# Block-sparse attention scores: six half-array matmuls over interleaved key parts become four whole-array matmuls over planes stacked in device memory

## The chip, the cores and the metric

The kernel runs on one core of one Trainium2 chip. Its time is device microseconds of one execution. Before the change, three runs took 908.22 us (median), 907.25 and 910.98 us.

## The reference, cut to what matters

One transformer layer on x of shape (16, 512, 128), float32: attention with 16 heads of 8 channels, then a mixture of four experts.

```python
qkv = (x @ qkv_w.T).reshape(B, N, 3, H, HD).transpose(2, 0, 3, 1, 4)    # x is layer-normed; H=16, HD=8, N=512
qb, kb = mean of q, k over blocks of 64 rows                            # M=8 blocks
c = einsum('bhmd,bhnd->bhmn', qb, kb) * SCALE
block_mask = (c >= top-1 of c) | eye(M)                                 # each query block sees its own and its best block
scores = where(mask, einsum('bhqd,bhkd->bhqk', q, k) * SCALE, -inf)
out = softmax(scores) @ v;  x = x + out @ proj_w.T + proj_b
x = x + experts(layernorm(x))      # 4 experts, hidden 512, top 2 by a router, gelu, gates by softmax
```

So each query block of 64 rows meets 128 keys: 64 of its own block and 64 of one selected block. Per batch row that is 8 blocks, each with 16 heads.

## The kernel before, in words

The 16 batch rows ("batches", b) are worked on in a software pipeline. During batch b's eight attention blocks m, TensorE also computes q, k and v for batch b+1 (`project`, L275), the router of b-1 (`c_route`) and the down projections of the experts of b-2 (`c_down`, L396: two chunks a block, numbers 2m and 2m+1). After block 7 come the sixteen up projections of the experts of b-1 (`c_up`), and behind number 13 of them `begin(b+1)` puts the first scores of the next batch. Everything is placed by hand: each engine has its program in order, and semaphores join them.

One block on TensorE goes: `weighted` (probabilities times values, L346), `row_max` (two transposes of block maxima, L326), `scores(b, m+1)` (L310), `shift` (16 small bf16 matmuls that add minus the row maximum, L335), other work, the `c_down` chunks (L403), `values(b, m+1)` (a transpose, L319). In blocks 0 and 7 chunk 2m stands ahead of the next scores and of the shift; in blocks 1 to 6 both chunks come near the end. `scores` of a block waits on the gelu of the bank that it overwrites for m below 2, and on the exponentials else. VectorE follows with `block_max` (L672, two a block) and `row_max` (L681), ScalarE with the exponential (L940), the gelus (L976) and copies.

Precision: q and k are each split into a high and a low float32r part, and a score is high*high + low*high + high*low. Before, `kv` holds for each channel (h, d) on its own partition, for 128 keys, three values side by side: high k, low k, v. `qdiag` holds q block-diagonally: partition (h, d) has numbers only in the columns of head h, eight heads to a half of the array. `scores` runs three products for each half: six matmuls with 64 partitions and 512 columns. SyncE places q with 32 DMAs a batch (`place_q`, L1143), 16 KB each.

The keys travel as follows. ScalarE and VectorE write k high, k low and v into `stage`. SyncE stores it in device memory as `table` (L1136) and copies it into the own half of `kv` (L1140). VectorE finds the best block (`a_select`) and writes row numbers (`index`, L647); GpSimd gathers those rows from `table` into `selected` (L1050); SyncE writes them to `chosen` (L1157) and reads them back, permuted, into the other half of `kv` (L1164). For batch 0 GpSimd gathers straight into `kv` with eight indirect DMAs (L1059), one a block, each with a semaphore of its own. SyncE runs all its DMAs in program order, and a wait in it holds what stands behind.

Of the kernel before, what the change touches and what calls it, by code (L numbers as in the profile page):

```python
# [32 lines left out]
ROW = 3 * BS  # L33
# [29 lines left out]
def layer(nc, x, wqkv_t, wproj_t, proj_b, w1, b1_t, w2, b2, wr, br, ident, head_sum,  # L63
          head_one, block_rank, row_mine, row_base, lane_base, expert_before, expert_rows, own_block, head_mask,
          query_rows, key_rows, out):
    with ExitStack() as ctx:
# [23 lines left out]
        rbase, lbase = sb("rbase", [P, 1]), sb("lbase", [P, 1])  # L90
# [18 lines left out]
        qdiag = [sb(f"qdiag{g}", [P, 2, HH, N // 2], F32R) for g in range(2)]  # L109
        stage = [sb(f"stage{i}", [P, M, BS, 3], F32R) for i in range(2)]  # L110
        kv = [sb(f"kv{i}", [P, M, KEYS, 3], F32R) for i in range(2)]
# [11 lines left out]
        first_index = sb("first_index", [P, M], U32)  # L123
# [49 lines left out]
        gates = [nc.dram_tensor(f"gates{b}", [E * T, P], F32, kind="Internal").ap() for b in range(B)]  # L173
        constant = nc.dram_tensor("constant", [E, D], F32, kind="Internal").ap()
# [10 lines left out]
        table_out = [sem(f"table_out{i}") for i in range(2)]  # L185
        own_in = [sem(f"own_in{i}") for i in range(2)]
        gathered, sel_out = sem("gathered"), sem("sel_out")
        sel_in = [sem(f"sel_in{i}") for i in range(2)]
        first_in = [sem(f"first_in{m}") for m in range(M)]
# [5 lines left out]
        constant_out = sem("constant_out")  # L195
# [34 lines left out]
        second = [(hsum, head_sum), (rank, block_rank), (mine_of, row_mine), (rbase, row_base), (lbase, lane_base), (wproj, wproj_t),  # L230
# [5 lines left out]
        PLACED = H * 16  # L236
# [7 lines left out]
        def taken(b):  # L244

            return 16 * (times(b, 2) - (1 if b % 2 == 0 else 0))
# [10 lines left out]
        def tensor(pe):  # L257
# [33 lines left out]
            def scores(b, m):  # L291
                j, i, u = b % 2, m % 2, b * M + m
                if m % HALF == 0:
                    pe.wait_ge(q_placed[m // HALF], PLACED * (b + 1))
                if m == 0:
                    pe.wait_ge(own_in[j], 16 * times(b, 2))
                    if b >= 1:
                        pe.wait_ge(sel_in[j], taken(b))
                if b == 0:
                    pe.wait_ge(first_in[m], 16)  # L300
                if m < 2 and b >= 2:
                    pe.wait_ge(gelued, UPS * (b - 2) + (UP_SPREAD if m == 0 else UPS))
                elif u >= 2:
                    pe.wait_ge(exped, u - 1)
                for n in range(3):
                    for half in range(2):
                        r = slice(half * P // 2, (half + 1) * P // 2)
                        keys = kv[j][r, m, :, 1 if n == 2 else 0]
                        queries = qdiag[m // HALF][r, 1 if n == 1 else 0, :, m % HALF * BS:(m % HALF + 1) * BS]
                        ins = pe.matmul(s_ps[i][:, half * N:(half + 1) * N].rearrange("p (h s) -> p h s", s=BS), keys, queries,  # L310
                                        start=n == 0, stop=False, skip_group_check=True)
                        if n == 2:
                            ins.then_inc(scored, 1)

            def values(b, m):
                was = bank_v.next("values", b, m)
                if was:
                    pe.wait_ge(bank_v.free, was)
                pe.transpose(v_ps[:, 0:P], kv[b % 2][:, m, :, 2].bitcast(F32), idn[:]).then_inc(bank_v.full, 1)  # L319
# [144 lines left out]
            for b in range(B):  # L464
                ahead = b >= 1 and b + 1 < B
                for m in range(M):
# [27 lines left out]
                    if b >= 2 and not edge:  # L494
                        c_down(b - 2, 2 * m)
# [64 lines left out]
        def vector(v):  # L560
# [39 lines left out]
            def a_q_parts(b):  # L600
                if b >= 1:
                    for g in range(2):
                        v.wait_ge(q_placed[g], PLACED * b)
# [3 lines left out]
            def a_k_low(b):  # L607
                st, kview = stage[b % 2], block_ap(a_ps[:])
                v.wait_ge(k_high, b - 1)
                total = step(v.tensor_reduce(ksum[:], kview, AXX, ALU.add))  # L610
                v.tensor_tensor(st[:, :, :, 1], kview, st[:, :, :, 0].bitcast(F32), ALU.subtract).then_inc(bank_a.free, 1)
                return total

            def a_k(b, bank="a"):
                j, (of, src) = b % 2, banks[bank]
                st, kview = stage[j], block_ap(src[:])
                v.wait_ge(of.full, of.at["k", b])
                if b >= 2:
                    v.wait_ge(table_out[j], 16 * times(b - 2, 2))
                    v.wait_ge(own_in[j], 16 * times(b - 2, 2))  # L620
                hi = step(v.tensor_copy(st[:, :, :, 0], kview))
                total = step(v.tensor_reduce(ksum[:], kview, AXX, ALU.add))
                v.wait_ge(dve_step, hi)
                v.tensor_tensor(st[:, :, :, 1], kview, st[:, :, :, 0].bitcast(F32), ALU.subtract).then_inc(of.free, 1)
# [8 lines left out]
            def a_select(b):  # L633
# [11 lines left out]
                if b >= 3:  # L645
                    v.wait_ge(gathered, 16 * (b - 2))
# [3 lines left out]
            def a_select_first():  # L650
                v.wait_ge(bank_a.full, bank_a.at["products", 0])
                v.tensor_scalar(crow[:].rearrange("p m n -> p (m n)"), a_ps[:, 0:M * M], 1.0 / (BS * BS), SCALE,
                                ALU.mult, ALU.mult).then_inc(bank_a.free, 1)
                v.wait_ge(bank_a.free, bank_a.at["products", 0])
                v.wait_ge(dve_step, step(v.tensor_reduce(cmax[:], crow[:], AXX, ALU.max)))
                v.wait_ge(dve_step, step(v.tensor_tensor(ceq[:], crow[:], heads_of(cmax[:]).broadcast_to([P, M, M]), ALU.is_ge)))
                counted = step(v.tensor_reduce(cties[:], ceq[:], AXX, ALU.add))
                ranked = step(v.tensor_tensor(crow[:], ceq[:], rank[:].rearrange("p (o n) -> p o n", o=1).broadcast_to([P, M, M]),
                                              ALU.mult))
                v.wait_ge(dve_step, ranked)  # L660
                v.wait_ge(dve_step, step(v.tensor_reduce(crank[:], crow[:], AXX, ALU.max)))
                v.tensor_scalar(first_index[:], crank[:], -float(P), lbase[:], ALU.mult, ALU.add).then_inc(index_done, 1)
                v.wait_ge(dve_step, counted)
                return step(v.tensor_reduce(ties[:, 0:1], cties[:], AXX, ALU.max))
# [145 lines left out]
            a_rows(1)  # L810
# [3 lines left out]
            a_q_parts(0)  # L814
            v.tensor_copy(idn16[:], idn[:]).then_inc(dve_set, 1)
            v.wait_ge(attention_in, SECOND)
            tied = a_select_first()
# [88 lines left out]
        def scalar(act):  # L906
# [6 lines left out]
            def a_v(b, bank="a"):  # L913
                j, (of, src) = b % 2, banks[bank]
# [642 lines left out]
```

## Time and profile before

| | us |
|---|---|
| median of three runs | 908.22 |
| profiled execution | 907.23 |
| its span, first to last instruction | 905.6 |
| TensorE busy | 861.6 (95%) |
| VectorE busy | 523.0 (58%) |
| ScalarE busy | 469.8 (52%) |
| GpSimd busy | 181.8 (20%) |
| DMA moved | 99.40 MB, 96021 packets |
| mean granted TensorE clock | 0.987 |

Busy time of TensorE is modelled from pipelined matmuls, so a stretch in which it is always busy need not be one in which it works at its peak. The chain of waits is the better guide: it gives each microsecond of the span to the instruction that the end waited for. The rows themselves stand in a section further down. The first scores of batch 0 start 28.26 us into the span, and after batch 1 every batch takes the same time.

### The profile page before, as it was taken

What the parts mean: (1) busy time and instruction counts of PE and PEld (TensorE: products, weight loads), DVE (VectorE), ACT (ScalarE), POOL (GpSimd) and SP (SyncE); (2) the same over time, 40 slices, a digit from 0 to 9 for tenths busy, and PEclk for the clock granted to TensorE, in tenths of its full rate; (3) what the DMA queues carried; (4) which work ended last, traced back from release to release, by engine and by line L of the source; (5) the groups of instructions that cost most, each with busy time, mean ns of one, the idle gap of its engine ahead of it and who ended that gap; (6) DMA issues with size and microseconds to landing.
All of it is one profiled execution on the core that took longest, in us unless ns stands there. A gap on an engine that the chain in (4) does not pass through costs nothing.

```text
span 905.6 us, 24229 instructions
## 1 busy us (share of the span) xinstructions
PE 861.6 (95%) x9638; PEld 578.9 (64%) x9638; DVE 523.0 (58%) x1525; ACT 469.8 (52%) x754; POOL 181.8 (20%) x183
## 2 busy tenths in 40 slices
PE   3887799999999999999999999999999999999995
PEld 2665576666667666666666666666766666666662
DVE  7545647565565756656474656556475755646321
ACT  1432374655547474654647465564746455473740
POOL 5701010312022121302112130312203130211111
PEclk9898999999999999999999999999999999999998
DMA  7440442425344351625435152534525262530110
GB/s 209 141 127 21 119 139 73 129 77 166 98 137 133 84 160 37 190 74 153 115 114 155 44 158 76 155 111 119 151 77 135 67 180 73 149 109 3 59 59 14
DMA packets 96021, 99.40 MB, mean 110 GB/s; under 512 B 8968, under 2 KB 82704, under 8 KB 95904
## 3 DMA queue, kind: packets, MB, share of 16 engines
q1 hardware_dynamic: 93168, 85.09, 33.6%
q0 software_dynamic: 2544, 12.58, 4.3%
q8 instruction: 78, 1.28, 0.6%
q14 instruction: 39, 0.32, 0.1%
q10 hardware_dynamic: 192, 0.13, 0.1%
HBM read 48.10 MB, written 28.71 MB: 85 GB/s over the span
## 4 chain that ended last, share of the span: by engine, by line
PE 88%; ACT 4%; DVE 3%; issue 1%; SPq 1%; DMA 1%; POOL 0%; POOLq 0%; DVEq 0%; ACTq 0%
PE y_ps L403 23%; PE s_ps L310 13%; PE o_ps L346 8%; PE s_ps L259 6%; PE s_ps L261 5%; PE s_ps L260 5%; PE s_ps L335 4%; ACT hid L976 4%; PE o_ps L353 4%; PE v_ps L326 3%; PE v_ps L319 2%; PE v_ps L365 2%; PE a_ps L376 2%; PE a_ps L268 2%; PE v_ps L403 2%; PE v_ps L360 2%
## 5 line engine op out<-in xcount | busy, mean ns | idle before, releaser
L403 PE MATMUL y_ps<-hid,w2s 128*128 128x512 f32 x480 | 235.1, 600 | 0.0
L672 DVE TRANSPOSE_TENSOR_REDUCE rmax<-s_ps 128x16 bf16<-128x512 f32 x256 | 168.9, 701 | 92.2 <-PE s_ps L310 89.8
L940 ACT ACTIVATE prob<-s_ps 128x1024 f32<-128x1024 f32 x128 | 131.3, 1026 | 173.6 <-PE s_ps L335 173.6
L976 ACT ACTIVATE hid<-s_ps,b1s 128x512 f32<-128x512 f32 x256 | 171.2, 689 | 36.9 <-PE s_ps L261 34.8
L310 PE MATMUL s_ps<-qdiag,kv 64*128 64x512 f32 x768 | 132.8, 451 | 1.9 <-DMA qdiag<-qpair 1.9
L1079 POOL TENSOR_TENSOR yT<-yT,gate_cols 128x512 f32<-128x512 f32 x48 | 61.5, 1282 | 304.1 <-DVE gate_cols L768 303.7
L259 PE MATMUL s_ps<-xnhi,w1hi 128*128 128x512 f32 x256 | 112.5, 439 | 1.5
L403 PEld LDWEIGHTS y_ps<-hid,w2s 128*128 128x128 f32 x480 | 83.0, 192 | 43.8 <-issue 40.0
L310 PEld LDWEIGHTS s_ps<-qdiag,kv 64*128 64x128 f32 x768 | 84.8, 252 | 28.4 <-ACT hid L976 10.6
L261 PE MATMUL s_ps<-xnhi,w1lo 128*128 128x512 f32 x256 | 100.9, 394 | 0.0
L681 DVE TENSOR_REDUCE nmax<-v_ps 128x64 bf16<-128x256 bf16 x128 | 54.0, 422 | 80.3 <-PE v_ps L326 79.7
L260 PE MATMUL s_ps<-xnlo,w1hi 128*128 128x512 f32 x256 | 100.3, 392 | 0.0
L346 PEld LDWEIGHTS o_ps<-prob,vaug 128*32 128x32 f32 x4096 | 63.4, 110 | 50.4 <-issue 37.1
L933 ACT COPY vaug<-v_ps 128x128 f32<-128x128 f32 x128 | 34.1, 266 | 117.3 <-PE v_ps L319 116.6
L346 PE MATMUL o_ps<-prob,vaug 128*32 128x64 f32 x4096 | 84.1, 223 | 0.1
L335 PEld LDWEIGHTS s_ps<-nmax,hone 64*128 64x128 bf16 x2048 | 37.5, 96 | 40.3 <-DVE nmax L681 22.9
L259 PEld LDWEIGHTS s_ps<-xnhi,w1hi 128*128 128x128 f32 x256 | 49.9, 195 | 18.9 <-ACT hid L976 8.8
L335 PE MATMUL s_ps<-nmax,hone 64*128 64x64 bf16 x2048 | 52.8, 192 | 3.5 <-DVE nmax L681 3.5
L948 ACT COPY oT<-o_ps 128x512 f32<-128x512 f32 x64 | 37.6, 587 | 34.9 <-PE o_ps L346 34.9
L261 PEld LDWEIGHTS s_ps<-xnhi,w1lo 128*128 128x128 f32 x256 | 48.0, 188 | 11.1
L260 PEld LDWEIGHTS s_ps<-xnlo,w1hi 128*128 128x128 f32 x256 | 48.5, 190 | 6.6 <-issue 0.7
L1041 POOL TENSOR_TENSOR xs<-xs,projb 128x512 f32<-128x512 f32 x16 | 20.5, 1282 | 140.2 <-DVE xn L579 140.2
(151 smaller groups left out, 1069.6 us busy)
## 6 DMA issues: line engine op xcount, KB each, us to landing
gate_cols<-gates SPq DMA_DIRECT2D x64, 256.0 KB, 4.3
kv_table<-stage SPq DMA_DIRECT2D x16, 768.0 KB, 3.9
kv<-stage SPq DMA_DIRECT2D x16, 768.0 KB
kv_chosen<-selected SPq DMA_DIRECT2D x15, 768.0 KB, 5.1
kv<-kv_chosen SPq DMA_DIRECT2D x15, 768.0 KB, 5.0
qdiag<-qpair SPq DMA_DIRECT2D x504, 16.0 KB
xs<-in_x SPq DMA_DIRECT2D x16, 256.0 KB, 5.6
out_x<-x SPq DMA_DIRECT2D x16, 256.0 KB, 5.9
```

The lines of the kernel that those rows point to most:

```text
L259: pe.matmul(dst, left_hi, right_hi, start=True, stop=False)
L260: pe.matmul(dst, left_hi, right_lo, start=False, stop=False)
L261: return pe.matmul(dst, left_lo, right_hi, start=False, stop=True)
L310: ins = pe.matmul(s_ps[i][:, half * N:(half + 1) * N].rearrange("p (h s) -> p h s", s=BS), keys, queries, start=n == 0, stop=False, skip_g ...
L335: ins = pe.matmul(s_ps[i][:, half * N + h * BS:half * N + (h + 1) * BS], hone[r, h, :], nmax[i][r, :], start=False, stop=True, skip_group_ ...
L346: ins = pe.matmul(o_ps[32 * (h % HQ):32 * (h % HQ) + VW, h // HQ, i * BS:(i + 1) * BS], vaug[i][:, h, :], prob[i][:, h, :], start=True, st ...
L403: ins = pe.matmul(dst[:], w2s[:, n, :], hid[:, n, :], start=(c == 0), stop=(c == C - 1))
L672: v.tensor_reduce(rmax[m % 2][:, :, half * P // 2:half * P // 2 + HH].rearrange("p k h -> p h k"), s_ps[m % 2][:, half * N:(half + 1) * N] ...
L681: v.tensor_reduce(nmax[m % 2][:].rearrange("h (b c) -> h b c", b=2), v_ps[:, 0:P].bitcast(BF16).rearrange("h (b g c) -> h b c g", b=2, g=4 ...
L940: act.activation(prob[m % 2][:].rearrange("p h s -> p (h s)"), s_ps[m % 2][:], ACT.Exp, scale=SCALE).then_inc(exped, 1)
L976: act.activation(hid[:, k, :], up_ps[up_bank(k)], ACT.Gelu, bias=b1s[:, k:k + 1]).then_inc(gelued, 1)
L1079: g.tensor_tensor(yT[:], yT[:], gate_cols[(E * b + e) % NG][:], ALU.add).then_inc(summed, 1)
```

## The change

Each row of `table` gets four planes per channel instead of three interleaved values: high k, low k, high k, v, 64 numbers each. On partitions, a quad of four heads now stands as (head, channel, plane), 4*8*4 = 128 partitions. q gets matching planes (high, high, low, zero) in a new table in device memory, `qtab`, so one matmul with 128 partitions sums all three products of four heads. A block takes four matmuls (one per quad) of 256 columns. The q, k and v of batch b+1 go through device memory: `put_q`, `place_q` (8 DMAs a batch of 128 KB), `put_high` and `put_low` (table in two parts), `take_own` (own keys read back from `table`), `take_keys` in two halves and `take_values`. v is kept apart in `vals`. `stage` has one buffer instead of two. Batch 0 takes the same way as the others; its eight direct gathers go. In blocks 1 to 6 of batches 2 and up, chunk 2m of `c_down` moves to between `scores(b, m+1)` and `shift(b, m)`; in block 0 it moves from ahead of the scores to behind them. The constants `head_sum`, `row_mine` and `row_base` are relabelled for the new order of rows.

```diff
+PLANES = 4
+ROW = PLANES * BS
@@ scores
-                for n in range(3):
-                    for half in range(2):
-                        r = slice(half * P // 2, (half + 1) * P // 2)
-                        keys = kv[j][r, m, :, 1 if n == 2 else 0]
-                        queries = qdiag[m // HALF][r, 1 if n == 1 else 0, :, m % HALF * BS:(m % HALF + 1) * BS]
-                        ins = pe.matmul(s_ps[i][:, half * N:(half + 1) * N]..., keys, queries, start=n == 0, ...)
+                if m % HALF == 0:
+                    pe.wait_ge(sel_k_in[j][m // HALF], 16 * times(b, 2))
+                for g in range(QUADS):
+                    queries = qdiag[m // HALF][:, g, :, m % HALF * BS:(m % HALF + 1) * BS]
+                    ins = pe.matmul(s_ps[i][:, g * HQ * BS:(g + 1) * HQ * BS]..., keys[j][:, m, g, :],
+                                    queries, start=g % 2 == 0, ...)
@@ values: waits at m == 0
+                    pe.wait_ge(own_v_in[b % 2], 16 * times(b, 2))
+                    pe.wait_ge(sel_v_in[b % 2], 16 * times(b, 2))
@@ order of a block on TensorE
-                    edge = m in (0, M - 1)
-                    if b >= 2 and edge:
-                        c_down(b - 2, 2 * m)
                     if m + 1 < M:
                         scores(b, m + 1)
+                    if b >= 2:
+                        c_down(b - 2, 2 * m)
                     shift(b, m)
...
-                    if b >= 2 and not edge:
-                        c_down(b - 2, 2 * m)
@@ sync, new functions
+            def put_high(b):
+                s.wait_ge(k_high, b + 1)
+                s.dma_start(plane_of(table[b], ..., 0, 1), stage[:, :, 1, :]).then_inc(table_out, 16)
+            def put_low(b, of_k, of_v):
+                s.dma_start(plane_of(table[b], ..., 1, PLANES), stage[:]).then_inc(table_out, 16)
+                s.dma_start(vals[b % 2][:, :, 0:BS], stage[:, :, 2, :]).then_inc(own_v_in[b % 2], 16)
+            def take_own(b):
+                s.wait_ge(table_out, 2 * 16 * (b + 1))
+                s.dma_start(keys[b % 2]...[:, :, 0:BS], key_rows_of(table[b])).then_inc(own_k_in[b % 2], 16)
+            def put_q(b):
+                s.dma_start(into[:, 0, :], qhi).then_inc(q_out, 16)
+                s.dma_start(into[:, 1:3, :], qpair[:]).then_inc(q_out, 16)
+            def place_q(b, half):
+                s.wait_ge(q_out, 2 * 16 * (b + 1))
+                for h in range(HQ):
+                    s.dma_start(qdiag[half][r, :, h, :], qtab[b % 2]...[h][:, :, half * N // 2:(half + 1) * N // 2]
+                                ).then_inc(q_placed[half], 16)
+            def put_selected(b):
+                s.wait_ge(gathered, 16 * (b + 1))
+                for half in range(2):
+                    s.dma_start(chosen[b][r, :], selected[r, :]).then_inc(sel_out[half], 16)
+            def take_keys(b, half):
+                s.wait_ge(sel_out[half], 16 * (b + 1))
+                s.dma_start(keys[b % 2][:, half * HALF:(half + 1) * HALF, :, BS:]...,
+                            key_rows_of(chosen[b][half * P // 2:(half + 1) * P // 2, :])).then_inc(sel_k_in[b % 2][half], 16)
+            def take_values(b):
+                s.dma_start(vals[b % 2][:, :, BS:], plane_of(chosen[b], ..., PLANES - 1, PLANES)).then_inc(sel_v_in[b % 2], 16)
+            def take_selected(b):
+                take_keys(b, 0)
+                take_values(b)
+                take_keys(b, 1)
@@ sync, order for batch b + 1 where b >= 1
+   put_q, put_high, place_q(half 0), put_low, take_own, put_selected, take_selected, place_q(half 1)
@@ sync, order for batch 0
+   q_null x2, load(third), put_high, put_low, put_q, take_own, place_q(half 0), put_selected, take_selected, place_q(half 1)
@@ vector, before the loop
+            v.memset(prob[0][:, 0:HH, :], 0.0).then_inc(null_set, 1)
-            a_rows(1)
             total = a_k(0, "y")
...
-            tied = a_select_first()
+            tied = a_select(0)
+            a_rows(1)
@@ scalar, before the loop
-            for h in range(HH, H):
-                act.dma_start(qdiag[0][r, :, h % HH, :], qpair[r, :, 0:N // 2]).then_inc(q_placed[0], 16)
@@ pool, before the loop
-            a_select_first()
+            a_select(0)
```

## Rows read from the trace of the kernel before

**Rows 1.** The page's chain of waits: shares of the span by engine

```profile
PE 88%; ACT 4%; DVE 3%; issue 1%; SPq 1%; DMA 1%; POOL 0%; POOLq 0%; DVEq 0%; ACTq 0%
```

**Rows 2.** Windows, one batch each: us, busy by engine, clock, DMA share, GB/s

```profile
439.00:491.00 52.00, 51.87 (x598) 34.62 (x598) 31.82 (x94) 29.20 (x48) 10.04 (x10) 1.00 0.42 118
491.00:543.00 52.00, 51.87 (x598) 34.63 (x598) 31.92 (x94) 29.21 (x48) 10.03 (x10) 1.00 0.41 118
```

**Rows 3.** Chain of waits in one batch, TensorE's pieces: start us, us, what

```profile
438.69 0.96 PE s_ps L310 x6
439.65 0.32 PE v_ps L319
...
441.49 0.91 PE y_ps L403 x2
442.40 0.96 PE s_ps L310 x6
443.36 0.25 PE s_ps L335 x16
...
447.82 0.54 PE a_ps L376 x4
...
453.56 0.23 PE a_ps L260
...
455.74 0.11 PE v_ps L319
...
476.81 0.34 PE s_ps L335 x16
```

**Rows 4.** ScalarE's timeline in that batch: start us, us, line, operation

```profile
440.70 1.38 ACT L976 ACTIVATE hid<-s_ps,b1s 128x512 f32<-128x512 f32 x2 [0.43 <-PE s_ps L261]
442.10 1.28 ACT L940 ACT_TABLE_LOAD   x1
```

**Rows 5.** VectorE's timeline in block 3 of that batch

```profile
459.73 0.69 DVE L610 TENSOR_REDUCE ksum<-a_ps 128x8 f32<-128x512 f32 x1 [0.77 <-ACT stage L926]
...
461.91 0.41 DVE L681 TENSOR_REDUCE nmax<-v_ps 128x64 bf16<-128x256 bf16 x1
```

**Rows 6.** Timelines of SyncE's queue and of GpSimd, same batch

```profile
465.59 0.36 SPq L1136 DMA_DIRECT2D kv_table<-stage  x1
...
476.59 0.58 SPq L1157 DMA_DIRECT2D kv_chosen<-selected  x1
...
483.81 0.38 SPq L1164 DMA_DIRECT2D kv<-kv_chosen  x1
...
471.03 1.11 POOL L1050 DMA_INDIRECT selected<-kv_table,index  x1 [7.69 <-DVE index L647]
```

**Rows 7.** Windows around single transfers, columns as in rows 2

```profile
6.00:8.00 2.00, 0.49 (x3) 0.52 (x4) 2.00 (x9) 0.00 (x0) 0.21 (x1) 1.00 0.27 54
441.00:447.00 6.00, 5.96 (x77) 3.79 (x77) 3.08 (x9) 4.13 (x6) 1.22 (x1) 1.00 0.87 259
...
472.00:476.00 4.00, 4.00 (x64) 2.64 (x63) 3.36 (x14) 1.29 (x2) 1.72 (x3) 1.00 0.71 224
477.00:482.00 5.00, 5.00 (x62) 3.54 (x55) 3.15 (x16) 4.28 (x7) 1.67 (x3) 1.00 0.65 167
...
18.00:23.00 5.00, 3.11 (x11) 2.98 (x12) 2.94 (x11) 0.00 (x0) 0.88 (x1) 1.00 1.02 311
```

**Rows 8.** The page: median us from issue to landing

```profile
kv_table<-stage SPq DMA_DIRECT2D x16, 768.0 KB, 3.9
...
kv<-kv_chosen SPq DMA_DIRECT2D x15, 768.0 KB, 5.0
```

**Rows 9.** Chain of waits at the start

```profile
10.02 5.08 DVE xn L579 x4
15.10 0.74 DVE stage L621
...
28.26 1.15 PE s_ps L310 x4
```

**Rows 10.** Windows of batches 0 and 1, columns as in rows 2

```profile
28.30:68.00 39.70, 35.86 (x548) 26.33 (x548) 22.46 (x52) 15.09 (x26) 12.51 (x14) 0.91 0.48 133
68.00:127.50 59.50, 47.94 (x595) 36.60 (x594) 33.29 (x114) 27.12 (x46) 8.73 (x11) 0.91 0.31 84
```

More of the change, by code:

```diff
@@ L242, in stages, with key_rows_of, plane_of @@
             return (2, 0, 1, 3) if b == 0 else (2, 3, 4, 5)
-        def taken(b):
-            return 16 * (times(b, 2) - (1 if b % 2 == 0 else 0))
+        def key_rows_of(dram):
+            return dram[:, :].rearrange("(n q) (r s) -> (q r) n s", q=HQ, s=BS)
+        def plane_of(dram, pattern, first, last):
+            return dram[:, :].rearrange(pattern, n=M, d=HD)[:, :, first * BS:last * BS]
         def heads_of(ap):
@@ L318, in values @@
                     pe.wait_ge(bank_v.free, was)
[L319 removed]
+                if m == 0:
+                    pe.wait_ge(own_v_in[b % 2], 16 * times(b, 2))
+                    pe.wait_ge(sel_v_in[b % 2], 16 * times(b, 2))
+                pe.transpose(v_ps[:, 0:P], vals[b % 2][:, m, :], idn[:]).then_inc(bank_v.full, 1)
             def row_max(b, m):
@@ L1155, in put_selected @@
-            def put_selected(b):
-                s.wait_ge(gathered, 16 * b)
-                s.dma_start(chosen[b][:, :].rearrange("(m h) c -> h m c", m=M), selected[:]).then_inc(sel_out, 16)
-            def take_selected(b):
-                j = b % 2
-                s.wait_ge(sel_out, 16 * b)
+                s.dma_start(vals[b % 2][:, :, 0:BS], stage[:, :, 2, :].bitcast(F32)).then_inc(own_v_in[b % 2], 16)
+            def take_own(b):
+                s.wait_ge(table_out, 2 * 16 * (b + 1))
+                if b >= 2:
+                    s.wait_ge(scored, 2 * M * (b - 1))
+                s.dma_start(keys[b % 2][:].bitcast(F32).rearrange("p m g k -> p (m g) k")[:, :, 0:BS],
+                            key_rows_of(table[b])).then_inc(own_k_in[b % 2], 16)
@@ L1162, in take_selected @@
+            def take_values(b):
+                for half in range(2):
+                    s.wait_ge(sel_out[half], 16 * (b + 1))
                 if b >= 2:
                     s.wait_ge(bank_v.full, bank_v.at["values", b - 2, M - 1])
-                s.dma_start(kv[j][:, :, BS:, :].bitcast(F32).rearrange("p m s c -> p m (s c)"),
-                            chosen[b][:, :].rearrange("(m h) (d c) -> (h d) m c", m=M, d=HD)).then_inc(sel_in[j], 16)
+                s.dma_start(vals[b % 2][:, :, BS:],
+                            plane_of(chosen[b], "(n h) (d c) -> (h d) n c", PLANES - 1, PLANES)).then_inc(sel_v_in[b % 2], 16)
@@ L1193, in sync @@
             load(second, attention_in)
+            s.wait_ge(null_set, 1)
+            for q_rows in qtab:
+                s.dma_start(q_rows.rearrange("(p t) c -> p t c", t=PLANES)[:, 3, :],
+                            prob[0][:, 0:HH, :].rearrange("p h s -> p (h s)")).then_inc(q_null, 16)
             load(third, experts_in)
-            a_v(0, bank_y, bank_v)
-            place_q(0, 0, range(HH))
-            place_q(0, 1, range(H))
+            put_high(0)
+            put_low(0, bank_y, bank_v)
+            put_q(0)
+            take_own(0)
+            place_q(0, 0)
+            put_selected(0)
+            take_selected(0)
+            place_q(0, 1)
             for b in range(B):
```

199 lines of the change are left out of this document (83 added, 116 removed).

## The prediction

> **What bounds the kernel now.** I read the chain of waits first: 88% of the span is TensorE's [rows 1]. Then the windows: from batch 2 on, a batch takes 52.0 us with TensorE busy throughout at the full granted clock, while VectorE and ScalarE work 32 and 29 us and DMA fills 0.42 of its time [rows 2]. So in the fourteen batches 2 to 15 a microsecond taken from TensorE is one gained, unless another engine or a transfer then comes late. Batches 0 and 1 (39.7 and 59.5 us) are looser and run partly at half clock [rows 10]. Ahead of them lie 28.3 us of start, in which TensorE waits for data [rows 9]. That gives three terms: start, batches 0 and 1, and fourteen steady batches.
>
> **Scores on TensorE.** Six half-array matmuls cost 0.96 us on the chain [rows 3]. The new four have 256 columns each, on all 128 partitions. No row shows that shape. From below: a full matmul of 512 columns costs 0.23 us when its weights load behind the one before (L260) [rows 3], and half the columns give 0.115, so 0.46 for four. From above: nothing gained, 0.96, if loads no longer hide. Four records that are almost nothing but a weight load (4 columns) take 0.54 us, 0.135 each (L376) [rows 3]. So load and stream are about equally long here; I take 0.125 a matmul, 0.50, and 0.09 for the first, whose load nothing hides behind the short transposes of `row_max`: 0.59. That saves 0.37 a block.
>
> **The chunk ahead of the shift.** It costs no work, but it parts two groups that both run on half arrays. The shift behind scores takes 0.25 us, behind a full-array chunk 0.34 [rows 3]: +0.09 in blocks 1 to 6. Net 0.28 x 6 = 1.68 us a batch. In exchange VectorE's row maximum has 1.45 us of cover instead of 0.96, and it needs about 0.5.
>
> The Trainium skill ("TensorEngine Tiling (Array Packing)", Key Properties) says that changing the tiling mode drains the array, which speaks against placing the chunk there. The row agrees in kind and prices it at 0.09 us. By the rule alone, without a figure, the sum would only be said to be smaller.
>
> **The first scores of a batch** stand between up projections, so their load hides: 0.50 for 0.96, and the transpose behind them needs no change of tiling, 0.11 for 0.32 [rows 3]. With block 0's second scores (-0.37 + 0.09) that is nominally 0.95 us. But `scores(b, 1)` overwrites the banks of the last gelus. These end at 442.08, and it started at 442.40 behind the chunk [rows 3, 4]. Now it comes first. The gelus move up by the 0.66 us that TensorE gained (last up projection 441.36 to 440.70), end at 441.43, and TensorE reaches the scores at 440.84. So 0.6 us of waiting appears, and the gain of this stretch is 0.35, not 0.95.
>
> **Block 3 to 4.** VectorE's `nmax` of block 4 starts at 461.91, delayed by the k sums, which started at 459.73 behind ScalarE's copy [rows 5], itself behind the exponential. The shift is later by the chunk (0.95) less 0.37, so that whole chain slides by some 0.6 us while the block gets shorter: shift 4 waits about 0.35 us more. In the other blocks the same sum leaves room.
>
> A steady batch: 1.68 + 0.35 - 0.35 = about 1.65 us less, 52.05 to 50.4. Bounds: 4.0 less if no wait appears and a matmul costs 0.115; 1.5 more if loads don't hide.
>
> **Transfers.** Price of a run, from engine time: 441 to 447 holds 3072 runs of 512 B, 6 x 0.87 x 16 / 3072 = 27 ns; 18 to 23 moves runs of 768 B at 311 GB/s, 39 ns; in 6 to 8 some 400 tiny runs come to about 9 ns each beside 128 of 512 B [rows 7]. Between them 256 B should cost about 18 ns; 9 and 27 are the bounds. Per batch: own keys 4096 runs, 4.6 us of all engines; selected keys the same in two halves; table, values and q some 8 us more. The busy share rises from 0.42 to about 0.66. That in itself costs nothing, but the last chain counts. Before, from the start of a batch (438.69): table written +26.9, gather +32.3, chosen written +37.9, read back +45.1 [rows 6], landed 5.0 later [rows 8] at +50.1; needed at +52.05. After: table +26.0, landed +30.2; own keys and gather (2.8 us of engine time for 0.79 MB, 4 x 0.71 [rows 7], so 3.8 for 1.05 MB) share the engines from +32 to +40.4; the chosen write (about 3.1 us of engine time, now 4.1 [rows 7]) lands by halves at +43.8 and +46; first keys +48.3, values +49.6. Needed at +50.4 and +50.9. It just fits, by 2.1 and 1.3 us. SyncE's waits: behind `take_own` wait q, `put_selected` and the gates; with 17 fewer DMAs a batch to issue (19 for 36) it is not the one that is late.
>
> **Start.** VectorE's a_rows(1) took 5.08 us ahead of the k split at 15.10 [rows 9]; moved behind it, k is ready from 11.5 and the index at about 19. The queue carries the weights and two q_null stores until 18. Then: table (1.3 + 2.5 us) at 22.3; own keys after values and q 25.5 to 30.5 with the gather; `place_q` 32; chosen 32 to 36, first half 34.5; keys 39.3, values 40. First scores at 39.5 instead of 28.26: +11.2 (bounds +7 and +18, by the price of a run). The direct gathers that go had let block 0 begin with an eighth of the keys.
>
> **Batches 0 and 1.** They have no chunk; 0.37 a block less, in part lost in waits at these clocks: -1.2 each (0 to -3).
>
> **Sum**, against the profiled execution of 907.2 (span 905.6 and 1.6 around it; 1.0 below the median): 907.2 + 11.2 - 2.4 - 14 x 1.65 = 892.9, so 893.
>
> **Rivals.**
> 1. *Late keys* (slower). With runs of 256 B at the price of 512 B (27 ns), own keys take 6.9 us, half the selected 3.5, values 1.7: +4.1 us, values at +53.7. TensorE then waits 2.8 us a batch, 53.2 us instead of 52.05: 907.2 + 8.8 + 14 x 1.15 = 932. It decides from a wait of 1.0 us a batch, where gain and start cancel. For it: the margin of 1.3 us is worked out, not seen. Against: two sizes and the tiny runs lie on one line.
> The Trainium skill ("DMA: Bandwidth & Descriptors", Specifications) gives 512 B as the least transfer at line rate, with read-modify-write below. This change cuts runs of 768 B into 256 B; no row here has enough of them to test it. By that rule this rival's price holds.
> 2. *Loads don't hide* (slower). Four times stream plus load, 0.115 + 0.115 each, is 0.92 and the scores gain nothing; with 0.09 x 6 and the waits, +1 a batch: 907.2 + 11.2 + 14 = 932. The row of 0.23 us for 512 columns speaks against it.
> The Trainium skill ("TensorE: Matmul & The Clock Gate", What overlaps and what doesn't) says that a weight load overlaps a matmul only where row groups differ. The up projections here, all on the full array, do overlap.
> 3. *All cover holds*: 0.46 a group, no new wait, 3 us a batch, start +9: 872.
> 4. *The gain turns into waits* of VectorE and ScalarE (the gelus and block 3 are two already), 0.5 to 0.9 us a batch: about 905.
>
> **Chances.** Forecast 0.42, late keys 0.24, loads 0.06, all cover 0.13, waits 0.15. Range 874 to 934; the likeliest case alone 883 to 902. About 0.5% is what can be told from no change: faster than 903.7 gets 0.42 + 0.13 + a fifth of rival 4 = 0.58, within 0.13, slower 0.29.
>
> **What would show it.** The scores group at 0.5 to 0.6 us; a wait of the first-block scores on a gelu of 0.6 us; the shift at 0.34; batch windows of 50.4 us; first scores near 39.5; DMA share near 0.66. I am wrong if a wait on `keys` or `vals` stands in the chain at each batch's begin, if the group stays near 0.96, or if the clock falls in those gaps.

## The result, and the profile after

| | median us | runs | lowest to highest |
|---|---|---|---|
| before, same chip | 909.23 | 4 | 907.25 to 910.98 |
| after | 925.58 | 4 | 918.75 to 930.87 |

The ratio is 1.0181, 95% interval 1.0146 to 1.0217: slower, by 1.5 to 2.2%. Forecast was 893, and faster. The profiled execution took 926.25 (span 924.6). First the page's chain of waits of the kernel after, shares of the span by engine, then its windows, one batch each (columns as in rows 2: us, busy by engine, clock, DMA share, GB/s).

```profile
PE 58%; DMA 26%; ACT 6%; DVE 4%; issue 3%; SPq 2%; POOL 0%; POOLq 0%; DVEq 0%; ACTq 0%
```

```profile
562.15:613.57 51.42, 50.01 (x581) 32.42 (x581) 31.71 (x94) 28.73 (x47) 10.04 (x10) 1.00 0.68 177
507.93:562.15 54.22, 52.80 (x580) 33.95 (x581) 31.80 (x94) 28.13 (x46) 10.04 (x10) 0.94 0.67 174
...
43.00:81.70 38.70, 34.49 (x533) 26.17 (x533) 21.84 (x52) 14.99 (x26) 0.97 (x1) 0.89 0.86 205
81.70:139.00 57.30, 45.43 (x570) 35.49 (x570) 33.01 (x112) 25.76 (x44) 8.73 (x11) 0.88 0.57 142
```

DMA is now 26% of the chain, from 1% [rows 1]. A share of the chain isn't time lost: it says what the end waited for, and most of that would have passed behind TensorE's work anyway. The steady batches take 51.4 to 51.8 us where keys are nearly or quite in time and up to 54.81 where they are late; before, all took 52.0 [rows 2]. TensorE is idle 1.4 us even in a good one. Measured from the first scores of one batch to those of the next, the span splits so:

| us | before | after | difference | forecast |
|---|---|---|---|---|
| start, to the first scores | 28.26 | 43.05 | +14.8 | +11.2 |
| batches 0 and 1 | 98.1 | 96.0 | -2.1 | -2.4 |
| batches 2 to 14 | 676.5 | 683.5 | +7.0 | -21.5 |
| batch 15 and the end | 102.8 | 102.1 | -0.7 | -1.6 |
| span | 905.6 | 924.6 | +19.0 | -14.3 |

Now the chain of waits inside a good batch of the kernel after (start us, us, what), which answers to rows 3.

```profile
562.31 0.54 PE s_ps L310 x4
562.86 0.11 PE v_ps L322
...
563.71 0.69 ACT hid L957
...
565.15 0.74 PE s_ps L310 x4
565.89 0.86 PE y_ps L406 x2
566.75 0.34 PE s_ps L338 x16
...
570.09 0.53 PE s_ps L310 x4
...
572.40 0.19 DVE logit L703
...
584.73 0.67 DVE gate_cols L750
...
585.44 1.13 PE y_ps L406 x2
```

Four scores matmuls take 0.53 us (0.96 before), the transpose behind them 0.11, the shift behind a chunk 0.34, and the second scores stand behind ScalarE's gelu. All of that was forecast. Not forecast are the two VectorE pieces: the column transposes now wait for the router's logits, and the chunk at 585.44, the first of an expert, waits for the gate columns of the one before. TensorE reaches both earlier relative to VectorE than it used to. The view of waits gives TensorE's idle time in this batch, 1.4 us in all (us in total, times, longest):

```profile
PE s_ps L310 <- ACT hid L957: 0.7, 1, 0.7
PE a_ps L273 <- DVE logit L703: 0.4, 1, 0.4
PE y_ps L406 <- DVE gate_cols L750: 0.3, 1, 0.3
```

The chain across the begin of the disturbed batch, and windows on it: 2.6 us with no matmul, then a granted clock of 0.66 and 0.75, with matmuls at 0.43 us (the 1.2 GHz level) where they took 0.23. The batch that ends with this wait took 3.4 us over 51.4, the one that begins behind it 2.8, so here the clock nearly doubled the price of a late key. It did so once. The keys were late by more than a microsecond at three other begins, with TensorE idle 1.43, 2.16 and 2.25 us before the scores at 192.53, 349.77 and 667.65 (2.93 us at 507.93); there the granted clock stayed at 1.00 and the next batch took 51.6 to 51.7.

```profile
496.84 4.32 DMA kv_chosen<-selected
...
501.18 6.50 DMA keys<-kv_chosen
...
507.93 0.71 PE s_ps L310 x4
...
510.38 0.43 PE s_ps L265
```

```profile
505.30:507.90 2.60, 0.00 (x0) 0.00 (x1) 0.00 (x0) 0.43 (x1) 0.00 (x0) 1.00 0.57 129
507.90:512.00 4.10, 3.49 (x13) 2.26 (x13) 1.75 (x3) 1.67 (x4) 0.00 (x0) 0.66 1.10 233
512.00:520.00 8.00, 7.99 (x87) 5.00 (x88) 2.86 (x7) 3.02 (x4) 1.28 (x1) 0.75 0.65 181
```

SyncE's queue and GpSimd's gather in the batch that begins at 401.49 (start us, us, engine, line, operation), which answer to rows 6:

```profile
428.68 0.38 SPq L1108 DMA_DIRECT2D kv_table<-stage  x1
...
432.66 0.73 SPq L1118 DMA_DIRECT2D keys<-kv_table  x1
443.63 1.12 SPq L1147 DMA_DIRECT2D kv_chosen<-selected  x2
447.95 0.38 SPq L1153 DMA_DIRECT2D keys<-kv_chosen  x1
450.54 0.36 SPq L1161 DMA_DIRECT2D vals<-kv_chosen  x1
```

```profile
433.87 1.11 POOL L1027 DMA_INDIRECT selected<-kv_table,index  x1 [7.57 <-DVE index L645]
```

From the batch's start: table issued +27.2 (forecast +26.0), gather issued +32.4 (+32), landed +42.1 (+40.4), first half of the chosen rows written +46.5 (+43.8), values issued +49.0 and landed +52.4 (+49.6). The lateness grows along the chain, from 0.4 us at the gather's issue to 2.8 at the values, and the margin was 1.3. In the batches that wait for keys the gather took 9.7 to 10.8 us and its rows were written out from +43.1 or later; here that was +42.1, and the batch took 51.63.

And the start, on the chain of waits (answers to rows 9):

```profile
15.15 5.83 DMA kv_table<-stage
...
21.84 12.20 DMA selected<-kv_table,index
...
34.62 6.30 DMA kv_chosen<-selected
```

### The profile page after: what moved, and what is told of

Read it like the earlier page. It is cut to its first block, busy times and chain, and to the rows that moved or that the text cites. A ratio compares the mean times of both kernels' runs of the same rounds, so it can differ in the third digit from the quotient of the medians.

```text
span 924.6 us, 23529 instructions
## 1 busy us (share of the span) xinstructions
PE 836.4 (90%) x9382; PEld 547.5 (59%) x9382; DVE 516.6 (56%) x1526; ACT 462.8 (50%) x754; POOL 175.0 (19%) x176
## 2 busy tenths in 40 slices
DMA packets 207441, 151.78 MB, mean 164 GB/s; under 512 B 123208, under 2 KB 189648, under 8 KB 203232
## 4 chain that ended last, share of the span: by engine, by line
PE 58%; DMA 26%; ACT 6%; DVE 4%; issue 3%; SPq 2%; POOL 0%; POOLq 0%; DVEq 0%; ACTq 0%
PE y_ps L406 17%; DMA selected<-kv_table,index 11%; DMA kv_chosen<-selected 6%; PE s_ps L310 6%; PE o_ps L349 5%; DMA kv_table<-stage 4%; ACT hid L957 4%; PE s_ps L338 4%; PE s_ps L264 3%; PE o_ps L356 3%; PE s_ps L266 3%; PE s_ps L265 3%; DMA vals<-kv_chosen 3%; PE a_ps L273 2%; DMA keys<-kv_chosen 2%
## 5 line engine op out<-in xcount | busy, mean ns | idle before, releaser
L406 PE MATMUL y_ps<-hid,w2s 128*128 128x512 f32 x480 | 248.7, 604 | 3.8 <-DVE gate_cols L750 3.7
L310 PE MATMUL s_ps<-qdiag,keys 128*128 128x256 f32 x512 | 95.4, 310 | 36.0 <-DMA keys<-kv_chosen 27.0
L310 PEld LDWEIGHTS s_ps<-qdiag,keys 128*128 128x128 f32 x512 | 71.4, 196 | 44.4 <-issue 31.9
L338 PEld LDWEIGHTS s_ps<-nmax,hone 64*128 64x128 bf16 x2048 | 37.8, 96 | 92.1 <-DVE nmax L663 55.3
L406 PEld LDWEIGHTS y_ps<-hid,w2s 128*128 128x128 f32 x480 | 77.7, 192 | 17.6 <-DVE gate_cols L750 6.7
L682 DVE TENSOR_TENSOR x<-v_ps,xs 128x128 f32<-128x128 f32 x64 | 18.5, 289 | 65.0 <-PE v_ps L368 64.8
```

What stands on the lines that cost most here:

```text
L310: ins = pe.matmul(s_ps[i][:, g * HQ * BS:(g + 1) * HQ * BS].rearrange("p (h s) -> p h s", s=BS), keys[j][:, m, g, :], queries, start=g % 2 ...
L338: ins = pe.matmul(s_ps[i][:, half * N + h * BS:half * N + (h + 1) * BS], hone[r, h, :], nmax[i][r, :], start=False, stop=True, skip_group_ ...
L406: ins = pe.matmul(dst[:], w2s[:, n, :], hid[:, n, :], start=(c == 0), stop=(c == C - 1))
```

## The experiments

Each ratio is to runs of the kernel before that were made beside that kernel's; their medians lie between 909 and 915.8 us, so absolute times of different lines compare only roughly. "First scores" and "steady" are read from each kernel's one profile, and "steady" is the sum over batches 2 to 14, with the shortest and longest of them. The profiled execution of e12 took 925.37 us, well over its median, so its times on the right are likely on the high side.

| run | us | ratio, 95% | first scores | steady | shortest, longest |
|---|---|---|---|---|---|
| before | 909.23 | 1 | 28.3 | 676.5 | 52.02, 52.09 |
| after | 925.58 | 1.018 (1.015 to 1.022) | 43.1 | 683.5 | 51.40, 54.81 |
| e1 | 965.60 | 1.054 (1.053 to 1.056) | 28.7 | 726.4 | 55.85, 56.10 |
| e2 | 899.37 | 0.983 (0.981 to 0.986) | 43.5 | 659.4 | 49.52, 52.01 |
| e3 | 905.21 | 0.989 (0.987 to 0.991) | 37.8 | 668.5 | 51.38, 51.62 |
| e4 | 885.06 | 0.969 (0.965 to 0.973) | 37.9 | 650.9 | 49.50, 50.38 |
| e5 | 914.43 | 0.998 (0.997 to 1.000) | 43.1 | 668.4 | 51.35, 51.62 |
| e7 | 925.76 | 1.011 (1.006 to 1.015) | 45.7 | 682.7 | 51.40, 54.21 |
| e9 | 876.88 | 0.959 (0.957 to 0.961) | 37.5 | 644.7 | 49.49, 49.75 |
| e10 | 894.65 | 0.978 (0.975 to 0.981) | 38.5 | 659.1 | 50.65, 50.90 |
| e11 | 897.87 | 0.985 (0.978 to 0.992) | 44.1 | 655.8 | 49.51, 52.16 |
| e12 | 916.72 | 1.007 (1.003 to 1.010) | 42.4 | 674.6 | 50.63, 53.32 |
| e13 | 916.90 | 1.008 (1.005 to 1.010) | 41.1 | 668.9 | 50.60, 53.07 |
| e14 | 962.86 | 1.058 (1.052 to 1.063) | 42.7 | 712.2 | 52.86, 57.32 |
| e15 | 888.39 | 0.969 (0.967 to 0.972) | 44.3 | 645.1 | 49.60, 49.67 |
| e16 | 903.44 | 0.988 (0.985 to 0.990) | 44.5 | 661.5 | 50.83, 51.16 |

**e1: the kernel before, with only the new order of the chunk.**

```
                     row_max(b, m)
...
-                    edge = m in (0, M - 1)
-                    if b >= 2 and edge:
-                        c_down(b - 2, 2 * m)
                     if m + 1 < M:
                         scores(b, m + 1)
+                    if b >= 2:
+                        c_down(b - 2, 2 * m)
                     shift(b, m)
```

> The kernel before with only the new place of the chunk: chunk 2m of the down projections stands behind the next scores and ahead of the shift. Theory (order): the chunk's new place makes waits of its own: block 0's second scores wait about 0.6 us on the last gelu, the normalised x's transposes about 0.4 us on the logits, the shift costs 0.09 us more in six blocks; +1.0 to +1.5 us a batch of 52.03, some +14 to +20 us in all. Rival (transfers only): the place is nearly free, +0.5 us a batch at most, under +8 us; all that the change loses, it loses in its transfers.

The order alone costs 50 us, far more than the 14 to 20 that I expected: 3.83 us in each of 13 batches. Its chain of waits:

```profile
583.36 1.03 PE s_ps L310 x4
584.39 1.06 PE y_ps L403 x2
585.45 0.34 PE s_ps L335 x16
```

A full-array chunk behind half-array scores takes 1.06 us (0.86 elsewhere), and the shift 0.34 instead of 0.25 [rows 3]: 0.29 for two changes of the array's mode, six times a batch, is 1.7 of the 3.8. TensorE sits idle another 1.3: 0.7 on the last gelus (two pieces of 0.69 before 583.36), 0.4 on the logits and 0.2 on ScalarE's copy of `attT` ahead of `values`. What is left, some 0.8, is not attributed. So the new order is a loss that the stacked scores only make smaller. (Batches 0 and 1, which have no chunk, took 6 us longer too, 104.3 for 98.1. The runs of the kernel before beside e1 were themselves 6.6 us longer than those whose profile is shown, 915.82 for 909.23, which would be as much; that it is this stays open.)

**e2: the stacked planes with the order of before.** The reverse of that edit, in the kernel after.

> The changed kernel with the chunk back where it was. Theory: an undisturbed batch falls from 51.4 us to about 49 (the scores group saves 0.43 us a block and the order's waits go), but the keys are late in nearly every batch then, since their chain takes about 51 to 52 us whatever TensorE does; total 912 to 920. Rival (order is neutral): 925 as the changed kernel. Rival (transfers are not a bound): 895.

0.983: faster than before, where the whole change is slower. It is also better than I expected (912 to 920, with batches of 49 and keys late in nearly all): the batches came out longer and the keys less late. In batches 2 to 14 the forecast missed 28.5 us; the old order gives back 24.1 of them. Batches of 50.4 us, which I had forecast for the new order, are those of the old one. With e3 and e4 below, 17.6 us of the 24.1 are the order itself (668.5 - 650.9) and 6.5 are keys that come less late (15.0 and 8.5 us of late keys).

**e3 and e4: keys that are never late.** The chosen keys and values are read from the table, before the gather's rows are written; the traffic is kept, the choice of blocks does not reach the scores. e3 has the new order, e4 the old.

```
-                s.wait_ge(sel_out[half], 16 * (b + 1))
...
-                            key_rows_of(chosen[b][half * P // 2:(half + 1) * P // 2, :])
+                            key_rows_of(table[b][half * P // 2:(half + 1) * P // 2, :])
...
-                    put_selected(b + 1)
                     take_selected(b + 1)
+                    put_selected(b + 1)
```

> The changed kernel, but selected keys and values are read from the table of own rows instead of from the chosen rows, ahead of the wait for the gather; the gather and the store of chosen rows still run with all their bytes. So the choice of blocks does not reach the scores (that part of the computation is left out), the traffic stays. Theory (late keys): every batch takes 51.4 us, the spread of 51.4 to 54.8 goes, some -15 us, and the first scores come near 33 us instead of 43; about 900. Rival (contention: traffic itself slows the engines or the start): batches stay at 52.5 on average and the total at 915 or more.

> As the one with keys read at once (the choice of blocks does not reach the scores), with the chunk back where it was. It shows what the four matmuls are worth when nothing is late. Theory: batches of 49.0 us, about 870. Rival (order is neutral): as the one with keys at once, about 900. Rival (the shift waits on the row maximum once the chunk no longer covers it): batches near 50.5, 888.

e3: every batch 51.4 us, one 51.6; late keys cost 683.5 - 668.5 = 15.0 us of the kernel after, 5 us at the start (first scores at 37.8, not near 33) and perhaps 4 in batches 0 and 1 (91.9 for 96.0). e4 against e3 gives the order's price without late keys: 17.6 us, 1.35 a batch. Of e4's expectations the rival with batches near 50.5 came nearest: they are of two kinds, 49.50 and 50.37, with one of 49.93. In the longer ones the chain goes through VectorE's row maximum in block 6:

```profile
506.36 0.53 PE s_ps L310 x4
506.88 0.40 PE s_ps L338 x16
...
510.18 1.09 PE v_ps L329 x2
...
511.29 0.44 DVE nmax L666
...
511.77 0.41 PE s_ps L338 x16
```

From 510.18 to the shift are 1.59 us, of which the transposes (0.22) and the scores (0.53) fill 0.75; 0.84 is waiting.

**e9: e4 with the new order in block 6 alone; e10: e3 with the old order in block 0 alone.**

```
                     if m + 1 < M:
                         scores(b, m + 1)
+                    if b >= 2 and m == 6:
+                        c_down(b - 2, 2 * m)
                     shift(b, m)
```

> The run with keys and values read from the table without a wait for the gather (the choice of blocks does not reach the scores), with the order of before, and in block 6 alone the new order (scores, chunk, shift). Its batches took 49.50 or 50.37 us, the longer ones with 1.09 instead of 0.22 us in front of the shift of block 6. Theory (there the shift waits for VectorE's row maximum, and a chunk ahead of it covers that): every batch takes about 49.5 us, the time falls by 3 to 6 us, ratio to before 0.962 to 0.966. Rival (the 0.87 us are something else and the chunk's own waits come on top): 50.4 us or more in every batch, ratio 0.970 or more.

> The run with keys and values read from the table without a wait for the gather (the choice of blocks does not reach the scores), with the new order, but block 0 as before (chunk, scores, shift). Theory (of the 1.0 to 1.9 us a batch that the new order costs, the wait of the scores of block 1 for the last gelu of the batch before, 0.6 us, is one term, and a chunk ahead of them covers most of it): batches of 51.0 us instead of 51.4, time down by 4 to 6 us, ratio to before 0.983 to 0.985 instead of 0.989. Rival (the cost lies wholly in blocks 1 to 6, where the chunk waits for the logit, the gate columns and the values): 51.4 us and 0.989.

e9: all batches 49.5 to 49.75, so one of the seven moved chunks does what the order could do at all. e10: 51.40 to 50.68; a chunk ahead of the second scores is worth 0.72, a little more than the gelu wait of 0.6 (the scores then also wait with their loads behind the gelu: 0.74 instead of 0.53 in the chain above). What remains of the order's price, 50.68 - 49.57 = 1.1 us, lies in blocks 1 to 5, where TensorE waits 0.4 us for the logits and 0.3 for the gate columns.

**e5: nearly no own keys to load.** From batch 2 on 2 of their 32 column groups are moved; the scores there use old own keys.

```
+                few = M * QUADS if b < 2 else 2
-                ... [:, :, 0:BS], key_rows_of(table[b])
+                ... [:, 0:few, 0:BS], key_rows_of(table[b])[:, 0:few, :]
```

> The changed kernel, but for batches 2 to 15 only 2 of the 32 column groups of the block's own keys are loaded back from the table (the scores there use old own keys); everything else, waits included, is as it was. Theory (the load of own keys slows the gather that runs beside it, and that makes the chosen keys late): the gather of batch 7 lands in 5.5 to 6.5 us instead of 9.7, the first keys land 3 to 4 us earlier, no block waits for keys from batch 2 on, every batch takes 51.4 us, and the time is about 911 us (ratio to before about 0.996; 0.98 of the changed kernel). Rival (the chain is late by the number of hops, each of them 4 to 6 us from issue to landing, and the load beside it matters little): the gather still takes over 8 us, keys late in some batches, ratio to before over 1.01.

Confirmed: 51.4 us in all batches but one of 51.62, and a ratio of 0.998 for 0.996. By itself e5 doesn't part the overlap from the bytes, since it moves 13.8 MB less; e15 below does. The profile's DMA issues over 190 to 720 us, first after, then e5 (count, median us from issue to landing):

```profile
selected<-kv_table,index POOLq DMA_INDIRECT x10, 9.7
```

```profile
selected<-kv_table,index POOLq DMA_INDIRECT x10, 5.8
```

**e11: e2 with the new order in block 6; e12: the same, own keys loaded behind the gather; e14: the kernel after with them there; e13: e12 with the experts' weights loaded last.**

```
-                    take_own(b + 1)
                     ...
                     put_selected(b + 1)
+                    take_own(b + 1)
                     take_selected(b + 1)
```

> The stacked planes of the changed kernel with the order of before, and in block 6 alone the new order (scores, chunk, shift); the chosen keys come by the real chain. Theory (one chunk, that ahead of the shift of block 6, covers VectorE's row maximum; the other seven of the new order cost): batches without late keys take 49.6 us, some batches still wait up to 2 us for keys, first scores at 43; 890 to 894 us where the old order alone had 899, ratio to before 0.973 to 0.977. Rival (a shorter batch only makes the keys late by as much, since their chain is as long as before): ratio 0.981 to 0.985, batches of 50.5 to 52 us with waits for keys.

> The kernel of the run before (old order, chunk ahead of the shift in block 6), with the load of the block's own keys issued behind the gather's landing and the two writes of the chosen rows, in every batch. Theory (the own keys share the DMA engines with the gather, which sets when the chosen keys land, and are not themselves in a hurry): the gather lands in 5.5 to 6.5 us as it did with nearly no own keys to load, no batch from 2 on waits for keys, first scores 1 to 4 us earlier, ratio to before 0.965 to 0.972. Rival (the same bytes now collide with the write and the load of the chosen keys, and the wait is only moved): the gather is fast, but writes and loads of the chosen rows take 3 to 4 us more between them, and the ratio stays at 0.973 to 0.977.

> The changed kernel, its new order in every block, with the load of the own keys issued behind the writes of the chosen rows. Theory (contention of own keys and gather makes the chosen keys late by about 15 us in all): batches of 51.4 us throughout, ratio to before 0.995 to 1.000, as with nearly no own keys to load. Rival (the wait is only moved to the chosen rows' write and load): ratio 1.010 to 1.018 as now, keys late in some batches by 1 to 3 us.

> As the run before, and the loads of the third group of constants behind the loads of the chosen keys of batch 0, with ScalarE's gelu of the hidden bias moved behind its exponentials of block 2. In the run with these loads behind the first queries the issue of them held SP's queue from 26.1 to 36.4 us (5.48 us for one of them alone), ahead of the writes of the gathered rows. Theory (that, and not the transfers, spoilt it): with the queue free first scores at 37 to 40 us, and the time 2 to 5 us below the run before. Rival (the experts' weights are then late in batch 0 and 1, GpSimd's gather for batch 1 behind their splitting too): first scores earlier by as much, but batches 0 and 1 longer by as much or more.

e11: where keys are in time its batches are 49.5, but others are late by up to 2.7, and the ratio is e2's within its interval. The rival holds: a shorter batch only uncovers the chain. e12 and e14 refute the cure that I had in mind, not the cause; both came out slower than even their rivals had it. The gather is fast again, 5.9 to 6.0 us, and then:

```profile
511.47 1.13 SPq L1147 DMA_DIRECT2D kv_chosen<-selected  x2
513.05 1.48 SPq L1118 DMA_DIRECT2D keys<-kv_table  x1
515.80 6.01 SPq L1153 DMA_DIRECT2D keys<-kv_chosen  x1
521.91 1.63 SPq L1161 DMA_DIRECT2D vals<-kv_chosen  x1
```

This is e14's SyncE queue. Issuing the chosen keys takes 6.01 us behind the own keys' 4096 runs, where it took 0.38; they land 8.6 us after issue, not 5.4, and every batch is late. By their ratios e14 and e1 are the slowest of all. e13 brings the first scores 1.3 us forward, to 41.1 and not to 37 to 40, and no time.

**e7: the experts' weights behind the first queries of batch 0**, in the kernel after.

> The changed kernel with the loads of the third group of constants (expert weights) issued behind the first half of the queries of batch 0 instead of ahead of the first table. Theory (the start is a queue of transfers and the 0.67 to 0.96 busy DMA engines set it): first scores 3 to 5 us before 43.05 us, so the ratio to before falls from 1.018 to about 1.013 to 1.015, if the first experts, which need these weights only in batch 1, do not wait. Rival (the start is a chain of landings, each of them latency): first scores at most 1 us earlier and the same time.

Wrong, and worse: first scores at 45.7. One of these loads took 5.48 us to issue where it had taken 2.40, in a stretch in which the DMA engines were full (27.5 to 33, share 1.09), and the writes of the gathered rows stood behind these loads until 36.4. SyncE's queue (start us, us, engine, line, operation):

```profile
27.53 5.48 SPq L1098 DMA_DIRECT2D hid<-in_b  x1
```

The ratio is below that of the kernel after, but their intervals touch and the medians are equal, so no gain is claimed.

**e15 and e16: keys and values projected before the queries**, so that the own keys are loaded ahead of the gather; e15 on e11, e16 on the kernel after.

```
-            return (2, 0, 1, 3) if b == 0 else (2, 3, 4, 5)
+            return (2, 0, 1, 3) if b == 0 else (4, 2, 3, 5)
...
+                    put_high(b + 1)
+                    put_low(b + 1, bank_a, bank_a)
                     take_own(b + 1)
+                    put_q(b + 1)
+                    place_q(b + 1, 0)
                     put_selected(b + 1)
```

> The stacked planes with the order of before and the new order in block 6 alone, and from batch 2 on keys projected in block 2, values in block 3 and queries in block 4 (before: queries, keys, values), with the table put and the own keys loaded some 5 us earlier, ahead of the gather, whose index still comes with the products in block 5; the queries' table and diagonal are then written beside the gather. Theory (it is the overlap with the own keys that makes the gather 9.7 us and the chosen keys late): the gather takes 6 to 7.5 us, keys are late in no or few batches, these take 49.6 us, and the ratio to before falls from 0.985 to 0.970 to 0.975. Rival (the bytes have only changed places: the queries' 1.75 MB now run beside the gather): gather over 8.5 us, keys late as before, ratio 0.983 or more.

> The changed kernel, its new order in every block, with keys and values projected before the queries from batch 2 on, as in the run before. Theory: no or few late keys, batches of 51.4 to 51.6 us, ratio to before 0.998 to 1.003 instead of 1.018. Rival: keys late as before, ratio 1.010 or more.

e15 in the batch that begins at 389.38:

```profile
408.75 0.36 SPq L1113 DMA_DIRECT2D kv_table<-stage  x1
...
412.69 0.74 SPq L1123 DMA_DIRECT2D keys<-kv_table  x1
...
425.88 1.12 SPq L1152 DMA_DIRECT2D kv_chosen<-selected  x2
430.54 0.39 SPq L1158 DMA_DIRECT2D keys<-kv_chosen  x1
433.37 0.39 SPq L1166 DMA_DIRECT2D vals<-kv_chosen  x1
```

```profile
389.38:438.98 49.60, 49.22 (x582) 32.88 (x581) 31.82 (x94) 28.64 (x47) 10.04 (x10) 1.00 0.77 192
```

All thirteen batches take 49.60 to 49.67. In this one the own keys go out at +23.3 (+31.2 in the kernel after), the gather at +29.9 (+32.4) and values at +44.0 (+49.0). Its gather took 6.6 us; from 190 to 720 us the median is 7.8, where e11 and the kernel after have 9.7. Against e11, from which e15 differs by this edit alone, the gather is issued no earlier (+29.9 in both), so it is the shorter gather that brings the keys in time. e15 is the fastest kernel that still computes everything: 0.969 of the kernel before, 3% faster, though its start is still 16 us longer. e16, with the new order, takes 22 us less in batches 2 to 14 than the kernel after, from late keys and also from waits (the one on the gate columns is gone): 0.988, better than the 0.998 expected. The bytes are the same in e11, e15, e16 and the kernel after (151.78 MB), so it was their place, not their sum.

## Why the prediction was wrong

The time went the other way than forecast, 16 us up instead of 14 down, and stayed inside the range only because that allowed for late keys or unhidden loads.

- **Scores on TensorE**: right, 0.53 to 0.54 for 0.59. What the Trainium skill says for rival 2 ("TensorE: Matmul & The Clock Gate", What overlaps and what doesn't), that a weight load overlaps only where row groups differ, does not describe this trace: four full-array matmuls whose loads have records of 0.19 us each (0.76 together) fit into 0.53.
- **The waits of a steady batch, the first step that failed.** "In the other blocks the same sum leaves room" put every wait but two at nothing. The good batch is 51.4 us instead of 50.4, 13 us of the miss. The table takes the chains of a batch before and of the good one after from one scores group to another; where the forecast expected only work, it found waits.

| from scores to scores of block | before | after | forecast | measured | what the chain shows |
|---|---|---|---|---|---|
| 0 to 2 | 7.92 | 7.78 | -0.35 | -0.14 | scores take 0.74, not 0.53, behind the gelu |
| 2 to 3 | 4.92 | 5.03 | -0.28 | +0.11 | wait for the logits |
| 3 to 4 | 5.12 | 4.80 | -0.28 | -0.32 | as forecast |
| 4 to 6 | 10.27 | 10.27 | -0.21 | 0.00 | copy, k sums, gate columns |
| 6 to 7 | 4.32 | 4.14 | -0.28 | -0.18 | small pieces |
| 7 to the next batch | 19.49 | 19.40 | -0.28 | -0.09 | small pieces |
| batch | 52.04 | 51.42 | -1.68 | -0.62 | |

I had looked for waits at the gelu (0.6 forecast, 0.72 by e10) and in block 3 to 4, and not asked who else is late when a chunk no longer stands between TensorE's transposes and VectorE: the logits, the gate columns, and in e1 `attT`. What the chunk's place costs in all was not mis-sized: the text charged it 7 x 0.09 + 0.6 + 0.35 = 1.58 us a batch, and e3 against e4 measures 1.35, e3 against e9 1.83. But the same text without these charges promises batches of 48.8 us to the old order, and the shortest measured are 49.5. The 0.09 was not the chunk's to pay: behind the full-array scores the shift takes 0.40 without a chunk between (e4's chain, 506.88) and 0.34 with it, where it took 0.25 before. So the stacked scores themselves bring a dearer shift, up to 0.15 in each of seven blocks, and the order of before was the better one with them all the same.

- **Transfers, the second.** The price of a 256 B run held. The windows of after from 434 to 442 (share 0.94) and of e5 from 434.2 to 441.3 (0.48) differ by 7.5 - 3.4 = 4.1 us of all engines, for 4096 runs less the few that e5 moves: 16 to 17 ns each. The trace's packet records say the same: the own keys are 1024 packets of four runs, 74 ns each, which is 18.5 ns a run and 4.7 us of all engines for 4.6 forecast. Rival 1 had 27 ns. What failed is the sum of hops: the gather's issue later by 0.4, gather 9.7 us for 8.4, the first half of the write 4.3 for 3.4. With a margin of 1.3 us worked out, all of it went. Rival 1 had the right mechanism and place but not its price. Late keys cost 15 us, in some batches and not in all, of which 2.8 is the one stretch at the lower clock. Its total, 932, is the nearest to 925, but rival 2 gave 932 as well (its sum leaves out the 2.4 of batches 0 and 1), with a mechanism that did not appear, so the nearness of the number says nothing.
- **Start**: +14.8 for +11.2. The write of the chosen rows took 6.3 us for 2.5 to the first half, the gather 12.2, with the own keys and the queries beside them.
- **Batches 0 and 1**: -2.1 for -2.4, which is luck. They took 96.0 us here, 91.9 in e3, whose keys are never late, and 102.0 in e5, which loads their keys as the kernel after does and whose batch 1 ran at a granted clock of 0.76 (0.88 in the kernel after). A term of 2 us can't be read from numbers that spread over 10.

The sum: 3.6 (start) + 0.3 + 13.0 (thirteen batches of 51.4 for 50.4) + 15.3 (what they take over 51.4: keys and clock) + 1.0 (batch 15) is 33.2, the distance from 892.9 to 926.25 to 0.2. It shares out the miss; what shows the causes are e2, e3, e4, e5 and e15.

## What to carry to other kernels

A work item moved from behind a short group to ahead of it is cover taken from every later consumer: list all engines' results that TensorE picks up after that point, and test the move block by block; here one of seven moved chunks wanted it. Count also what a new shape does to its neighbour: the full-array scores were as fast as hoped, and the shift behind them dearer. A chain of dependent transfers with a worked-out margin of 1 us in 50 has no margin; find what runs beside its slowest hop and start that earlier, not later.

## What the runs showed of the hardware

- Issuing a DMA can hold SyncE's queue while earlier transfers are under way: 6.01 us instead of 0.38 behind 4096 runs of 256 B (e14), 5.48 instead of 2.40 (e7).
- An indirect gather of 1 MB takes 5.8 us nearly alone (e5), 7.8 beside the queries' writes (e15), 9.7 beside the own keys' load (the kernel after; medians), and 12.2 at its start.
- Runs of 256 B cost 16 to 18.5 ns of a DMA engine each (the kernel after and e5).
- A full-array group behind a half-array one is dearer by 0.20 us (1.06 for 0.86), a half-array shift costs 0.25, 0.34 or 0.40 behind half-array scores, a chunk, or full-array scores.
- TensorE's granted clock fell to 0.66 and 0.75 over the 12 us behind one idle stretch of 2.9 us, and the two batches around it took 6.2 us over 51.4; behind three others, of 1.43, 2.16 and 2.25 us, it stayed at 1.00 (the kernel after).
